# Third layer of a decoder: one drive in four of the state-space scan made by GpSimd, and its cross attention rewritten as one stage in slots

## The chip, the cores and the metric

The kernel runs on one core of one Trainium2 chip. Its time is the device time of one launch in microseconds (us). Engine names here are those of the profile: PE is TensorE, DVE is VectorE, ACT is ScalarE, POOL is GpSimd and SP is SyncE. PSUM is the memory that matmuls write, SBUF the other on-chip memory. POOL has no operand in PSUM anywhere in this kernel.

## The reference

A decoder of four layers works on `x` of 16 batches x 128 tokens x 128 features, with a context of 16 x 120 x 96. Each layer has a mixing block, a cross attention and a feed-forward block, and after each block `x = layernorm(x + block(x))`. The change touches two blocks of the third layer, L2:

```python
# L2_attn: selective state-space model, D_MODEL 128, D_INNER 256, D_STATE 64
x, z   = split(x @ in_proj)                 # x goes through a causal convolution, then silu
dt     = softplus(low_rank(x) @ dt_proj_w + dt_proj_b)
B, C   = two more projections of the input, 64 columns each
h_t[d,n] = exp(dt_t[d] * A[d,n]) * h_{t-1}[d,n] + (dt_t[d] * u_t[d]) * B_t[n]     # for each state n
y_t[d]   = sum_n h_t[d,n] * C_t[n] + D[d] * u_t[d]
out    = (y * silu(z)) @ out_proj
# L2_xattn: cross attention, 16 heads of 64
q, k, v = x @ Wq, ctx @ Wk, ctx @ Wv        # 1024 columns each
out     = softmax(q k^T / 8) v @ Wo + bo
```

## The kernel before

All work is in float32, apart from the split B and C rows of the state-space block, which are three bfloat16 parts. The 16 batches are taken in NG = 4 groups of G = 4 batches (4 x 128 tokens = 512 columns, `GT`). A *stage* is a block in which every engine runs its own instruction list, in order, and the lists meet only through semaphores; between two stages all engines meet.

**`l2_attn`** is one stage. Features lie on partitions, so one state n of one group is a tile of 128 x 1024 (two halves of D_INNER x 512 columns, `HW` = 1024). The stage walks k = 0 to 255 (group g = k // 64, state n = k % 64), and for each k:

- PE copies row n of B over 128 partitions into the PSUM bank `b_bank`, and row n of C into `c_bank` (`row(k, m)`, L3173), and adds the `read` tile of k - 2 into the PSUM total through an identity matmul (`add`, L3182).
- DVE multiplies `b_bank` by `du` (dt times u, in SBUF) into two PSUM banks, `drive_` (L3372), and then scans along the columns, `scan` (L3380): `state = decay * state + drive`. The scan reads `decay` from SBUF and the drive from PSUM.
- ACT moves the C row to SBUF (`c_move`, L3299, two buffers) and makes `exp(dt * a)` two states ahead (`decay_`, L3292, three buffers).
- POOL multiplies the scanned state by the C row (`read_`, L3477), from SBUF to SBUF.

In between, at fixed n, stand the pieces that finish the group before and prepare the next. On DVE: `skip` at n = 2 (L3388, twice), `moments` at n = 10 (L3394, L3398, L3400), `scale` at n = 12 (L3405), `split_rest` at n = 28, 31, 34 and 37 (L3357), `softplus_` at n = 52 (L3362: it reads two tiles, both in SBUF). On POOL: `gated` at n = 2, `rstd_` at 10, `split_low` at n = 29, 32, 35 and 38, and `delta_u` at 53.

**`l2_xattn`** first loads its weights in a stage of its own (`load`), then clears two tiles in another, then runs a hardware loop over the four groups. In one pass these stages follow each other: transposes of x and a copy of the context (`load_group`, `context_group`), projections (a stage with L1271 for q, L1273 for k and L1276 for v, c = 0 to 7), the attention core of 16 units of 4 heads each (scores L1227, maximum L323, subtraction L327, exponential L347, transposes of the weights L296, values L307, reciprocal and division L332 and L334), transposes of the output (L229), the output projection (L253, L256) and the layer norm (`finish_group`). K is kept with zeros in the other head's half, so that a score matmul uses 128 rows for one head's 64. V has a column of ones, from which the sum of the weights comes.

## Time and profile before

| what | value |
|---|---|
| median of three runs | 5960.31 us (5947.09 to 5963.47) |
| the profiled execution's own time | 5968.24 us |
| its span in the profile | 5966.5 us |
| busy in the span | PE 4702.8 us, DVE 4159.5, ACT 2844.0, POOL 2449.2 |
| mean granted clock of TensorE | 0.888 |

The profile is of one execution. The span is the time from its first instruction to its last, and the run's own time lies 1.7 us above it. The twelve blocks follow one another, so each block's time counts in full. The busy shares above are averages over blocks with different limits, and what an engine's time is worth has to be read inside the block.

### The profile page before, as it was taken

Reading aid. Unit: us, or ns where it says so; the run is one execution under the profiler, and the core shown is the slowest. Engines: PE = TensorE matmul, PEld = TensorE weight load, DVE = VectorE, ACT = ScalarE, POOL = GpSimd, SP = SyncE. Lnnn points to the kernel's source line nnn. Section 1 sums busy time; section 2 is a strip of 40 time slices with the busy share of each in tenths; the row PEclk is TensorE's granted clock in tenths of the full one; section 3 lists DMA queues with packets and bytes.
Section 4 is the critical chain, followed back from the end, with each engine's and each line's share of the span. In section 5 each row is a group of like instructions: output and inputs, shape, how many; then the busy total and the mean of one; then the engine's idle time right before and its main releaser. Section 6 shows DMA issues by size and latency. Waiting matters only on the chain. (4 is left out here: it accounts for less than half of the span.)

```text
span 5966.5 us, 85422 instructions
## 1 busy us (share of the span) xinstructions
PE 4702.8 (79%) x29391; PEld 2817.2 (47%) x29392; DVE 4159.5 (70%) x7865; ACT 2844.0 (48%) x4658; POOL 2449.2 (41%) x2180
## 2 busy tenths in 40 slices
PE   8768999999999999579537667666886689826667
PEld 5555666666666666237412222223563444304444
DVE  3338888888888887574459999996453446557545
ACT  2326777777777776444235454542233235413211
POOL 0137666767666665340546666662002210001100
PEclk8779999999999999778569999998897779966788
DMA  0000000000000000000000000000000000002000
GB/s 15 6 27 9 1 18 4 1 20 1 20 1 20 1 5 1 4 2 2 3 7 0 0 0 0 0 0 13 0 0 13 12 8 5 1 11 60 6 23 7
DMA packets 74746, 49.73 MB, mean 8 GB/s; under 512 B 27816, under 2 KB 68921, under 8 KB 73593
## 3 DMA queue, kind: packets, MB, share of 16 engines
q1 hardware_dynamic: 72313, 43.71, 2.8%
q8 instruction: 221, 3.62, 0.3%
q0 software_dynamic: 2048, 1.05, 0.1%
q14 instruction: 164, 1.34, 0.1%
HBM read 40.11 MB, written 1.18 MB: 7 GB/s over the span
## 5 line engine op out<-in xcount | busy, mean ns | idle before, releaser
L3477 POOL TENSOR_TENSOR l_attn_read<-l_attn_state,l_attn_c_rows 128x1024 f32<-128x1024 f32 x256 | 604.5, 2361 | 329.3 <-DVE l_attn_state L3380 328.4
L2354 POOL TENSOR_TENSOR l_ffn_t<-l_ffn_t 128x512 f32<-128x512 f32 x384 | 488.5, 1272 | 520.6 <-DVE l_ffn_t L2221 520.6
L3380 DVE TENSOR_TENSOR_SCAN l_attn_state<-l_attn_decay,psum 128x1024 f32<-128x1024 f32 x256 | 584.9, 2285 | 8.1
L1954 PE MATMUL psum<-l_ffn_wq,l_ffn_xsT 128*128 128x512 f32 x1152 | 562.7, 597 | 22.0 <-DVE l_ffn_t L2221 13.4
L3182 PE MATMUL psum<-l_attn_read,ident 128*128 128x512 f32 x1024 | 495.2, 606 | 5.4 <-DVE l_attn_yz L3388 3.0
L3173 PE MATMUL psum<-l_attn_parts,pick 96*128 96x512 bf16 x512 | 200.8, 396 | 309.9 <-DVE psum L3372 309.9
L2365 POOL TENSOR_TENSOR l_ffn_p<-l_ffn_p,l_ffn_sm 128x512 f32<-128x512 f32 x384 | 399.6, 1041 | 61.9 <-DVE l_ffn_sm L2253 45.5
L2360 POOL TENSOR_TENSOR l_ffn_t<-l_ffn_t,l_ffn_ss 128x512 f32<-128x512 f32 x384 | 400.9, 1044 | 0.7 <-DVE l_ffn_ss L2236 0.7
L3299 ACT COPY l_attn_c_rows<-psum 128x512 f32<-128x512 f32 x256 | 149.9, 586 | 469.2 <-PE psum L3173 467.7
L3372 DVE TENSOR_TENSOR psum<-psum,l_attn_du 128x1024 f32<-128x1024 f32 x256 | 315.6, 1233 | 32.4 <-POOL l_attn_du L3454 4.6
L2217 DVE TENSOR_TENSOR l_ffn_t<-psum,l_ffn_tab 128x512 f32<-128x512 f32 x384 | 263.4, 686 | 105.4 <-ACT l_ffn_sq L2101 103.6
L2118 ACT COPY l_ffn_pT<-psum 128x512 f32<-128x512 f32 x384 | 224.6, 585 | 217.5 <-PE psum L1984 214.1
L2112 ACT ACTIVATE l_ffn_p<-l_ffn_p 128x512 f32<-128x512 f32 x384 | 241.4, 629 | 150.7 <-DVE l_ffn_p L2244 148.3
L3173 PEld LDWEIGHTS psum<-l_attn_parts,pick 96*128 96x128 bf16 x512 | 50.0, 98 | 553.7 <-DVE psum L3372 480.9
L2240 DVE TENSOR_REDUCE l_ffn_mx<-psum 128x4 f32<-128x512 f32 x384 | 258.1, 672 | 68.4 <-PE psum L1975 66.3
L203 POOL TENSOR_SCALAR rstd<-mean_var 128x4 f32<-128x4 f32 x12 | 2.8, 231 | 734.9 <-DVE mean_var L192 734.9
L3292 ACT ACTIVATE l_attn_decay<-l_attn_dt,l_attn_a 128x1016 f32<-128x1016 f32 x256 | 292.7, 1144 | 11.8 <-DVE l_attn_state L3380 11.4
L1998 PEld LDWEIGHTS psum<-l_ffn_pT,l_ffn_v 128*64 128x64 f32 x3072 | 160.1, 136 | 280.3 <-issue 173.8
L1608 ACT ACTIVATE l_attn_pT<-psum 128x512 f32<-128x512 f32 x320 | 173.6, 594 | 243.1 <-PE psum L1506 170.6
L2101 ACT ACTIVATE l_ffn_sq<-psum 128x512 f32<-128x512 f32 x384 | 230.6, 600 | 121.1 <-PE psum L1954 121.1
L1975 PE MATMUL psum<-l_ffn_kT,l_ffn_qT 64*128 64x128 f32 x3072 | 274.9, 297 | 0.0
L2244 DVE TENSOR_TENSOR l_ffn_p<-psum,l_ffn_mx 128x512 f32<-128x512 f32 x384 | 265.6, 692 | 13.2
(884 smaller groups left out, 11896.1 us busy)
## 6 DMA issues: line engine op xcount, KB each, us to landing
l_ffn_wq<-in_L_ffn_Wqkv SPq DMA_DIRECT2D x6, 1536.0 KB, 6.6
l_xattn_toep<-s4d_taps SPq DMA_DIRECT2D x4, 2048.0 KB, 17.4
l_ffn_wo<-in_L_ffn_Wo SPq DMA_DIRECT2D x6, 512.0 KB, 8.3
l_ffn_w<-in_L_ffn_W SPq DMA_DIRECT2D x6, 341.0 KB
l_ffn_w<-in_L_ffn_w SPq DMA_DIRECT2D x3, 512.0 KB, 5.8
l_attn_k<-l_attn_dense_k POOLq DMA_DIRECT2D x64, 16.0 KB, 1.8
l_attn_q<-l_attn_dense_q SPq DMA_DIRECT2D x64, 16.0 KB
l_xattn_conv_y<-l_xattn_conv_rows SPq DMA_DIRECT2D x64, 16.0 KB, 2.2
```

The source lines that it names most:

```text
L1954: nc.tensor.matmul(ring[it % 2], xsT[:, n % 2, m % G, :], wq[:, z, i * 512:(i + 1) * 512], start=True, stop=True).then_inc(itemed, 1)
L1975: last = nc.tensor.matmul(S[:, par, i, :], qT[r, m % G, 2 * c + i, :], kT[r, m % G, 2 * c + i, :], start=False, stop=True, skip_group_chec ...
L2217: nc.vector.tensor_tensor(t1[:, m % G, i, :].rearrange("p (h d) -> p h d", d=dh), dots.rearrange("p (h d) -> p h d", d=dh), rows(tab[:, z, ...
L2244: nc.vector.tensor_tensor(p_[:, k % 4, :, :].rearrange("p (i par) t -> p par i t", par=2), S, mx[:, k % 2, :, :].unsqueeze(3).to_broadcast ...
L2354: nc.gpsimd.tensor_tensor(t1[:, m % G, i, :], t1[:, m % G, i, :], t2[:, x % 3, :], ALU.add).then_inc(added, 1)
L2360: nc.gpsimd.tensor_tensor(t1[:, m % G, i, :].rearrange("p (h d) -> p h d", d=dh), t1[:, m % G, i, :].rearrange("p (h d) -> p h d", d=dh), ...
L2365: nc.gpsimd.tensor_tensor(p_[:, k % 4, :, :], p_[:, k % 4, :, :], col(sm[:, k % 4, :], T), ALU.mult).then_inc(weighted, 1)
L3182: last = nc.tensor.matmul(total[:, h * GT:(h + 1) * GT], K.ident[:], read[:, k % 3, h * GT:(h + 1) * GT], start=(n == 0), stop=(n == N - 1 ...
L3292: nc.scalar.activation(decay[:, k % 3, :, :, 1:T], dt[:, g % 2, :].rearrange("p (h g t) -> p h g t", h=2, g=G)[:, :, :, 1:T], ACT.Exp, sca ...
L3372: nc.vector.tensor_tensor(drive.rearrange("p (h n) -> p h n", h=2), rows(b_bank, 2), du[:, g % 2, :].rearrange("p (h n) -> p h n", h=2), A ...
L3380: nc.vector.tensor_tensor_scan(state[:, k % 3, :], decay[:, k % 3, :, :, :].rearrange("p h g t -> p (h g t)"), drive, 0.0, ALU.mult, ALU.a ...
L3477: nc.gpsimd.tensor_tensor(read[:, k % 3, :].rearrange("p (h n) -> p h n", h=2), state[:, k % 3, :].rearrange("p (h n) -> p h n", h=2), row ...
```

## The change

In `l2_attn`, for states with n % 4 == 2 (16 per group, 64 in all) the drive is no longer made by DVE. PE makes the B row in `c_bank` (`b_row_copied`), ACT moves it to SBUF (`b_move`), POOL multiplies it by `du` into a new SBUF tile `drive_sb` (`drive_here`), and the scan of that state takes its drive from there. `drive_here(k + 2)` stands on POOL right behind `read_(k)` with k % 4 == 0. Nothing else in the stage is changed.

```diff
+        by_pool = lambda k: k % N % 4 == 2
```

On PE (`b_row` and `c_row` are what `row(k, 0)` and `row(k, 1)` were):

```diff
+                def b_row_copied(k, c_done):
+                    g, n = k // N, k % N
+                    if n < 3:
+                        wait_parts(g)
+                    if c_done:
+                        pe.wait_ge(c_moved, c_done)
+                    nc.tensor.matmul(c_bank, K.pick3[:, n % SU:n % SU + 1].to_broadcast([96, 128]), parts[:, g % 2, n // SU, :],
+                                     start=True, stop=True).then_inc(b_copied_ready, 1)
...
-                    if k + 1 < NS:
-                        row(k + 1, 0)
+                    if k + 1 < NS and not by_pool(k + 1):
+                        b_row(k + 1)
                     if k >= 2:
                         add(k - 2)
                     if k + 1 < NS:
-                        row(k + 1, 1)
+                        c_row(k + 1)
+                    if k + 3 < NS and by_pool(k + 3):
+                        b_row_copied(k + 3, k + 2)
```

On ACT, and then on DVE:

```diff
                     c_move(k)
+                    if k >= 1 and k + 2 < NS and by_pool(k + 2):
+                        b_move(k + 2)
                     if k + 2 < NS:
                         decay_(k + 2)
...
-                    dve.wait_ge(driven, k + 1)
+                    p = pool_index(k)
+                    if by_pool(k):
+                        dve.wait_ge(pool_driven, p + 1)
+                    else:
+                        dve.wait_ge(driven, dve_index(k) + 1)
...
-                    nc.vector.tensor_tensor_scan(state[:, k % 3, :], decay[:, k % 3, :, :, :].rearrange("p h g t -> p (h g t)"), drive, 0.0,
+                    nc.vector.tensor_tensor_scan(state[:, k % 3, :], decay[:, k % 3, :, :, :].rearrange("p h g t -> p (h g t)"),
+                                                 drive_sb[:, p % 2, :] if by_pool(k) else drive, 0.0,
                                                  ALU.mult, ALU.add).then_inc(scanned, 1)
...
-                    drive_(k)
+                    if not by_pool(k):
+                        drive_(k)
```

On POOL:

```diff
+                def drive_here(k):
+                    g, p = k // N, pool_index(k)
+                    pool.wait_ge(b_copied, p + 1)
+                    pool.wait_ge(du_ready, g + 1)
+                    if p >= 2:
+                        pool.wait_ge(scanned, prior_pool(prior_pool(k)) + 1)
+                    nc.gpsimd.tensor_tensor(drive_sb[:, p % 2, :].rearrange("p (h n) -> p h n", h=2), du[:, g % 2, :].rearrange("p (h n) -> p h n", h=2),
+                                            rows(b_rows[:, p % 2, :], 2), ALU.mult).then_inc(pool_driven, 1)
...
                     read_(k)
+                    if k >= 1 and k + 2 < NS and by_pool(k + 2):
+                        drive_here(k + 2)
```

On DVE, in the state-space stage, before (L3372 makes a drive, the L3380 rows are scans; both write or read the drive in PSUM):

```order
L3372 TENSOR_TENSOR psum<-psum,l_attn_du 128x1024
L3380 SCALAR_TENSOR_TENSOR l_attn_state<-l_attn_decay,psum 128x1024
L3372 TENSOR_TENSOR psum<-psum,l_attn_du 128x1024
L3380 SCALAR_TENSOR_TENSOR l_attn_state<-l_attn_decay,psum 128x1024
L3372 TENSOR_TENSOR psum<-psum,l_attn_du 128x1024
```

And of the change at the same place (L3640 is the drive, L3652 the scan), for k = 4j + 1, 4j + 2 and 4j + 3:

```order
L3640 TENSOR_TENSOR psum<-psum,l_attn_du 128x1024
L3652 SCALAR_TENSOR_TENSOR l_attn_state<-l_attn_decay,psum 128x1024
L3652 SCALAR_TENSOR_TENSOR l_attn_state<-l_attn_decay,l_attn_drive_sb 128x1024
L3640 TENSOR_TENSOR psum<-psum,l_attn_du 128x1024
L3652 SCALAR_TENSOR_TENSOR l_attn_state<-l_attn_decay,psum 128x1024
```

The drive of 4j + 2 is gone from DVE, and the scan behind it has both its inputs, `decay` and `drive_sb`, in SBUF.

On POOL, at the start of the same stage, of the change (L3722 is `split_low`, L3729 `delta_u`, L3762 `drive_here`, L3752 `read_`; before, 30 `read_` follow the `delta_u` without a break):

```order
L3722 TENSOR_TENSOR l_attn_parts<-l_attn_rest,l_attn_low 32x512 x4
L3729 TENSOR_TENSOR l_attn_du<-l_attn_dt,l_attn_xz 128x1024
L3762 TENSOR_TENSOR l_attn_drive_sb<-l_attn_du,l_attn_b_rows 128x1024
L3752 TENSOR_TENSOR l_attn_read<-l_attn_state,l_attn_c_rows 128x1024 x5
L3762 TENSOR_TENSOR l_attn_drive_sb<-l_attn_du,l_attn_b_rows 128x1024
L3752 TENSOR_TENSOR l_attn_read<-l_attn_state,l_attn_c_rows 128x1024 x4
```

The second `drive_here` stands behind `read_(4)` and ahead of `read_(5)`, and so on every fourth.

`l2_xattn` becomes one stage for all four groups. A slot t works on the pair of heads c = t % 8 of group t // 8 for all four batches (32 pairs; slots from -3 to 36). Scores use 64 rows of PE for each head, the two heads of a pair in two PSUM banks (`score`, 8 matmuls). The softmax keeps queries on partitions; the weights are normalised on POOL before they are transposed (`weigh`), and the value matmul writes the output transposed, so that the transposes of L229 fall away. The next group's q, k and v projections are spread over the slots, one of each per slot. The layer norm's multiply and add move from DVE to POOL (`norm`). The tiles that had to be cleared are gone, and the weights are loaded in the same stage.

```diff
-        with nc.Fori(0, NB // G) as i:
-            b0 = i * G
-            load_group(K, b0)
-            context_group(K, b0)
...
-            core()
-            wide_out(K, o, oT, wo, bo[:])
-            finish_group(K, b0)
...
+        def misc_at(t):
+            out = []
+            for g in range(NG):
+                u = t - CH * g + 2
+                if 0 <= u < CH:
+                    out += [("q", g, u), ("k", g, u), ("v", g, u)]
+            for g in range(NG):
+                if t == CH * g - 3:
+                    out.append(("x", g))
+                if t == CH * g + 11:
+                    out.append(("fin", g))
+            return out
```

Each engine's slot, in the order of its list: PE does value(t - 3), the q projection, score(t), the k projection, turn(t - 2), the v projection, and then "x" or "fin". ACT does move_out(t - 3), the moves of q and k, move(t - 2, 0) and move(t - 2, 1), the moves of v and x, exp(t, 0) and exp(t, 1). DVE does sums(t - 1) (two reduce_sum of 128 x 480 and a reciprocal), then shift(t, 0) and shift(t, 1) (reduce_max and subtraction each). POOL does weigh(t - 1) (two multiplications of 128 x 480). The waits that tie them:

```diff
+                def score(n):
+                    g, c = divmod(n, CH)
+                    if n:
+                        pe.wait_ge(shifted, 2 * n)
...
+                def turn(n):
+                    pe.wait_ge(weighted, 2 * n + 2)
+                    if n:
+                        pe.wait_ge(p_moved, 2 * n)
...
+                def value(n):
+                    g, c = divmod(n, CH)
+                    pe.wait_ge(p_moved, 2 * n + 2)
+                    if n:
+                        pe.wait_ge(o_moved, n)
...
+                    for b in range(G):
+                        for z in range(2):
+                            last = nc.tensor.matmul(O[half(z), b * T:b * T + T], v[:, g % 2, b, (2 * c + z) * dh:(2 * c + z + 1) * dh],
+                                                    pT[:, n % 2, z, b * T:b * T + T], start=True, stop=True, skip_group_check=True)
+                    last.then_inc(o_done, 1)
```

"fin" is the output projection of a group: 32 matmuls of 128 x 128.

On PE, in the cross attention, one slot of the change (L1329 `value`, L1348 q, L1305 `score`, L1351 k, L1316 `turn`, L1355 v; x8 stands for eight matmuls):

```order
L1329 MATMUL psum<-l_xattn_pT,l_xattn_v 64x128 x8
L1348 MATMUL psum<-xT,l_xattn_wq 128x512
L1305 MATMUL psum<-l_xattn_k,l_xattn_q 128x120 x8
L1351 MATMUL psum<-ctxT_all,l_xattn_wk 128x480
L1316 MATMUL psum<-ident,l_xattn_p 120x128 x8
L1355 MATMUL psum<-l_xattn_wv,ctxT_all 120x512
```

Before, 24 projections stand together in front of the core, and one unit of the core is this:

```order
L1227 MATMUL psum<-l_xattn_kT,l_xattn_qT 128x2x120 x2
L296 MATMUL psum<-ident,l_xattn_l2x_p 120x128 x4
L307 MATMUL psum<-l_xattn_v,l_xattn_l2x_pT 128x65 x4
L1227 MATMUL psum<-l_xattn_kT,l_xattn_qT 128x2x120 x2
L296 MATMUL psum<-ident,l_xattn_l2x_p 120x128 x4
```

A slot stands for two units. The projections now lie between its parts.

## Rows read from the trace of the kernel before

**Rows 1.** Stretches: length, busy of PE, PEld, DVE, ACT, POOL, granted clock, DMA.

```profile
3109.00:4073.00 964.00, 661.47 (x1691) 255.00 (x1692) 927.61 (x572) 479.14 (x594) 633.70 (x282) 0.98 0.00 0
4114.00:4472.00 358.00, 300.08 (x1648) 227.42 (x1648) 199.44 (x412) 113.80 (x196) 5.07 (x8) 0.91 0.00 0
```

**Rows 2.** Timeline (start, duration, engine, line, names) of one state-space step.

```profile
4062.09 2.37 POOL L3477 TENSOR_TENSOR l_attn_read<-l_attn_state,l_attn_c_rows 128x1024 f32<-128x1024 f32 x1 [1.30 <-DVE l_attn_state L3380]
4062.11 1.23 DVE L3372 TENSOR_TENSOR psum<-psum,l_attn_du 128x1024 f32<-128x1024 f32 x1
4063.38 2.29 DVE L3380 TENSOR_TENSOR_SCAN l_attn_state<-l_attn_decay,psum 128x1024 f32<-128x1024 f32 x1
...
4063.63 1.88 PE L3182 MATMUL psum<-l_attn_read,ident 128*128 128x512 f32 x4
...
4065.74 2.35 POOL L3477 TENSOR_TENSOR l_attn_read<-l_attn_state,l_attn_c_rows 128x1024 f32<-128x1024 f32 x1 [1.29 <-DVE l_attn_state L3380]
...
4065.77 1.23 DVE L3372 TENSOR_TENSOR psum<-psum,l_attn_du 128x1024 f32<-128x1024 f32 x1
```

**Rows 3.** Timeline at n = 52, where DVE's `softplus_` meets a running `read_`.

```profile
3300.14 2.35 POOL L3477 TENSOR_TENSOR l_attn_read<-l_attn_state,l_attn_c_rows 128x1024 f32<-128x1024 f32 x1 [1.30 <-DVE l_attn_state L3380]
...
3301.31 2.27 DVE L3362 SCALAR_TENSOR_TENSOR l_attn_dt<-l_attn_dt,l_attn_tmp 128x1024 f32<-128x1024 f32 x1
```

**Rows 4.** The four instances of line L3362: shortest, median, longest in ns.

```profile
L3362 DVE SCALAR_TENSOR_TENSOR l_attn_dt<-l_attn_dt,l_attn_tmp x4: 1226/2270/2282, 3102.3 to 3787.9; 128x1024 f32<-128x1024 f32 x4
```

**Rows 5.** Timeline in the second layer: POOL's L3017 releases DVE's L2939.

```profile
2531.73 1.04 POOL L3017 TENSOR_TENSOR rstd<-rstd,minus_half 128x4 f32<-128x4 f32 x1
...
2532.74 1.27 POOL L3024 TENSOR_TENSOR l_attn_read<-l_attn_state,l_attn_c_rows 128x512 f32<-128x512 f32 x1
...
2532.87 1.75 DVE L2939 TENSOR_SCALAR x_all<-y,mean_var,rstd 128x128 f32<-128x128 f32 x3
```

**Rows 6.** DVE's groups of instructions in the state-space stage (count | busy us, mean ns).

```profile
L3357 DVE TENSOR_TENSOR l_attn_rest<-psum,l_attn_parts 96x512 f32<-96x512 f32 x13 | 8.8, 678 | 1.3 <-POOL l_attn_parts L3447 1.3
...
L3388 DVE SCALAR_TENSOR_TENSOR l_attn_yz<-l_attn_xz,l_attn_cl,psum 128x512 f32<-128x512 f32 x8 | 5.6, 741 | 4.5 <-PE psum L3182 4.5
L3398 DVE BATCH_NORM_STATS2 stats<-y 128x6 f32<-128x128 f32 x16 | 4.7, 294 | 0.5
```

**Rows 7.** Timeline: first instructions of the cross attention, and the next block's first.

```profile
4091.63 0.34 SPq L92 DMA_DIRECT2D l_xattn_wq<-in_L_xattn_Wq  x1
...
4101.94 3.52 DVE L1253 MEMSET l_xattn_v<- 120x4160 f32 x1 [12.35 <-PEq L42]
...
4117.70 2.05 PE L1271 MATMUL psum<-xT,l_xattn_wq 128*128 128x512 f32 x2 [2.07 <-PEq L39]
...
4473.03 0.35 SPq L92 DMA_DIRECT2D l_ffn_gate<-in_L_ffn_gate_w  x1
```

**Rows 8.** Timeline of projections in the third group: two turns of q, k and v.

```profile
4303.67 1.02 PE L1271 MATMUL psum<-xT,l_xattn_wq 128*128 128x512 f32 x2
...
4306.19 1.02 PE L1271 MATMUL psum<-xT,l_xattn_wq 128*128 128x512 f32 x2
```

**Rows 9.** Timeline of PE in the first layer's feed-forward block, which runs in slots.

```profile
1800.06 0.66 PE L1998 MATMUL psum<-l_ffn_pT,l_ffn_v 128*64 128x128 f32 x8
...
1800.65 0.66 PE L1960 MATMUL psum<-ident,l_ffn_t 128*128 128x128 f32 x4
...
1802.31 0.71 PE L1975 MATMUL psum<-l_ffn_kT,l_ffn_qT 64*128 64x128 f32 x8
...
1802.96 0.66 PE L1984 MATMUL psum<-ident,l_ffn_p 128*128 128x128 f32 x4
...
1803.45 1.88 PE L1954 MATMUL psum<-l_ffn_wq,l_ffn_xsT 128*128 128x512 f32 x4
```

**Rows 10.** Timeline of the output projection in the third group, one batch.

```profile
4368.25 2.02 PE L253 MATMUL psum<-l_xattn_wo,l_xattn_oT 128*128 128x128 f32 x16 [1.27 <-PEq L42]
```

**Rows 11.** DVE's groups of instructions in the cross attention (count | busy us, mean ns).

```profile
L327 DVE TENSOR_TENSOR l_xattn_l2x_p<-psum,l_xattn_l2x_max 128x480 f32<-128x480 f32 x64 | 42.1, 658 | 2.2
```

More of the change, by code:

```diff
@@ L1250, in l2_xattn @@
-        with stage(nc) as (block,):
+        wo = sb("wo", [128, CH, D])
+        bo = sb("bo", [128, D])
+        x_bias = sb("x_bias", [128, G, D])
+        q = sb("q", [128, CH, GT])
+        k = sb("k", [128, CH, KEYS])
+        v = sb("v", [NC_, 2, G, E])
+        p_ = sb("p", [128, 3, 2, G, NC_])
+        mx, sm = sb("mx", [128, 2, G]), sb("sm", [128, 2, 2, G])
+        pT = sb("pT", [NC_, 2, 2, GT])
+        oT = sb("oT", [128, 2, CH, GT])
+        st, mv = sb("st", [128, G, 6]), sb("mv", [128, G, 2])
@@ new lines, in l2_xattn @@
+        rs, nb = sb("rs", [128, G]), sb("nb", [128, G])
+        xT = K.xT[:].rearrange("p g t -> p (g t)")
+        O = K.bank[4]
+        spare = [K.bank[5 + i] for i in range(3)]
+        half = lambda z: slice(64 * z, 64 * z + 64)
+        def misc_at(t):
[10 more added lines that the diff above has]
+            return out
@@ new lines, in sums, with moments @@
+                def sums(n):
+                    for z in range(2):
+                        dve.wait_ge(exped, 2 * n + z + 1)
+                        if n >= 2:
+                            dve.wait_ge(weighted, 2 * (n - 2) + 2)
+                        nc.vector.reduce_sum(sm[:, n % 2, z, :], p_[:, n % 3, z, :, :], AX).then_inc(summed, 1)
+                    dve.wait_ge(summed, 2 * n + 2)
+                    nc.vector.reciprocal(sm[:, n % 2, :, :], sm[:, n % 2, :, :]).then_inc(recip, 1)
+                def moments(g):
+                    key = ("fin", g)
+                    wait_filled(dve, *key)
+                    dve.wait_ge(x_biased, g + 1)
+                    if g:
+                        dve.wait_ge(x_ready, g)
+                    nc.vector.tensor_tensor(K.y[:].rearrange("p g d -> p (g d)"), bank_of(key), x_bias[:].rearrange("p g d -> p (g d)"),
+                                            ALU.add).then_inc(moved[use[key] % 3], 1)
+                    wait_moved(dve, *key)
+                    for b in range(G):
+                        step(nc.vector.bn_stats(st[:, b, :], K.y[:, b, :]))
+                    if g:
+                        dve.wait_ge(rstd_ready, g)
+                    for b in range(G):
+                        nc.vector.bn_aggr(mv[:, b, :], st[:, b, :]).then_inc(var_ready, 1)
@@ L3196, in _ @@
                     dt_dot(0, h)
-                row(0, 0)
-                row(0, 1)
+                b_row(0)
+                b_row_copied(2, 0)
+                c_row(0)
                 for k in range(NS + 2):
                     g, n = k // N, k % N
-                    if k + 1 < NS:
-                        row(k + 1, 0)
+                    if k + 1 < NS and not by_pool(k + 1):
+                        b_row(k + 1)
                     if k >= 2:
@@ L3483, in _ @@
                 delta_u(0)
+                drive_here(2)
                 for k in range(NS):
```

284 lines of the change are left out of this document (227 added, 57 removed).

## The prediction

> **What bounds the kernel now.** I read the busy times of the two blocks first, then the timeline of one step in each. In the state-space steps DVE is busy 927.6 of 964 us [rows 1]; the reader is to see that no other engine is near that (PE 661, POOL 634, ACT 479). The timeline shows why: drive 1.23 us, scan 2.29 us, next drive, with gaps of 0.04 and 0.10 us between [rows 2]. One step is 3.66 us from drive to drive (4062.11 to 4065.77), four are 14.64. POOL starts its `read_` 0.07 us after a scan and is done 1.3 us before the next one is. So time taken off DVE here shortens the block, until POOL's chain is the longer one.
>
> The cross attention takes from 4091.63, where its first load is issued, to 4473.03, where the next block's first is [rows 7]: 381.4 us. Until 4117.70 it only loads, clears and transposes. In its four groups PE is busy 300 of 358 us and no other engine over 200 [rows 1]. PE has pauses only between stages. So what counts is PE's work, and the empty starts and ends of stages.
>
> **The state-space stage, step by step.** In words the change takes 64 drives of 1.23 us off DVE, which with their gap would be 64 x 1.37 = 88 us. I follow one cycle of four states, time 0 being the end of scan(4j), with the durations and gaps of [rows 2].
>
> - POOL: `read_(4j)` 0.07 to 2.43, `drive_here(4j + 2)` 2.39 to 4.75. It has no row of its own; I take 2.36 us, that of `read_`, which has the same shape and the same two SBUF inputs, one repeated over halves. Then `read_(4j + 1)` from 4.71, since its scan has long ended.
> - DVE: drive(4j + 1) 0.10 to 1.33, scan(4j + 1) 1.37 to 3.66. Then it waits for POOL's drive, until 4.82. That is the first loss: 1.16 us of the 1.37 gained.
> - The second loss is larger. scan(4j + 2) now has both inputs in SBUF, and starts 0.1 us behind a POOL instruction that reads SBUF. The trace has this pair: `softplus_` (two SBUF inputs) takes 1226 ns alone and 2270 ns in the middle of three others [rows 4]. At 3301.31 it starts while POOL's `read_` runs, until 3302.49; it ends at 3303.58, 1.09 us later [rows 3]. So it does nothing until POOL has finished, and then needs 0.14 us less than alone. Ordinary drives and scans, with one SBUF input, are not lengthened by a running `read_` [rows 2].
> - Who comes first is also in the trace. In the second layer POOL ends L3017 at 2532.77; its next instruction has already started, at 2532.74, while the DVE instruction that waited for L3017 starts at 2532.87, and its three operations end at 2534.62, 0.61 us behind that next POOL instruction (2534.01) [rows 5]. Here it is the same: `read_(4j + 1)` at 4.71, the scan at 4.82. So scan(4j + 2) waits to 7.07 and ends at 7.07 + 2.29 - 0.14 = 9.21.
> - Then two ordinary steps: 9.21 + 2 x 3.66 = 16.53. POOL is at rest before the next cycle starts, so it repeats.
>
> A cycle costs 16.53 - 14.64 = +1.89 us. For 63 of them (in the first, drive_here(2) is made ahead of everything) that is +119 us, and -1 in the first. What comes back: DVE now idles 3.4 us before every scan(4j + 2), and the pieces that stand there cost nothing: `skip` (2 x 0.74), `moments` (4 x 0.29, and about 1.1 for its addition and aggregations), two of four `split_rest` (0.68 each) [rows 6]. That is 4.9 us less overlaps of 0.1, 3 times: -14.5. At n = 32 `split_low` stands between `drive_here` and `read_`; there the scan already waits when POOL passes on, goes first, and saves 1.2 us, 3 times: -3.6. Sum of this stage: **+100 us**.
>
> The Trainium skill speaks against this change (SBUF — State Buffer, "Who interferes with whom"): a DVE instruction with two SBUF inputs contends with a GpSimd instruction that reads SBUF, and whichever issues first holds the shared ports for its whole length. By that rule, the trace agrees, with 2270 against 1226 ns. Without the rule the scan would start at 4.82, and the cycle be 14.42 us.
>
> PE, ACT: the B row for POOL costs PE 0.4 and ACT 0.6 us per cycle, and both have the room (PE 661 and ACT 479 of 964 us busy [rows 1]). PE's list is in order, and `b_row(4j + 4)` waits for drive(4j + 3), which ends at 10.54, so PE idles some 5 us in each cycle and then works through one copy of B, two additions of 1.9 us [rows 2] and three more copies. Worked through with the gaps above, the C row for `read_(4j + 4)` is moved at 14.0 (needed at 16.6), the B row for drive(4j + 5) is there at 14.9 (16.6), POOL's B row at 15.3 (18.9). I charge nothing; the cover is 1.7 us or more.
>
> **The cross attention.** PE's work per slot, start to start, each f32 matmul being two instructions except the transposes:
>
> - q, k, v: 2.52 us (4303.67 to 4306.19) [rows 8].
> - value, 16 instructions: eight of this kind take 0.59 us up to the next, of which 0.2 is the change of shape; 0.59 + 8 x 0.055 = 1.03. Scores, 16 of 64 rows: 0.65 + 8 x 0.063 = 1.15. Eight transposes: 0.49 + 4 x 0.11 = 0.93 [rows 9].
> - Changes of shape behind the projections: 0.17. Sum 5.8 us.
>
> `value(t - 3)` waits for ACT's second move of the slot before. The turn begins at 4.0, its halves are moved one after another, and the second is done at about 5.9: 0.1 us of wait. **5.9 us** a slot. The others stay below: DVE 2 x (0.66 + 0.66) + 2 x 0.66 + 0.2 = 4.2 by [rows 11]; ACT eight instructions of 0.6, 4.8; POOL 2 x 1.1, `read_`'s duration at 480 of 1024 columns.
>
> Start: DVE's first instruction behind the loads is at 4101.94 [rows 7], and PE no longer waits for the clearing; I put the first q at 4100.5. There q took 2.05 us for 1.02 later [rows 7, 8], so slots -2 and -1 cost 8 us instead of 5. Slots 0 to 2: 13.5, since they bring only part of the work but each score waits for the maximum and subtractions of the last. Slots 3 to 29: 27 x 5.9 = 159. Three output projections of 64 instructions in them: 2.02 us per 16 as read [rows 10], and a little less start to start, 3 x 7.7 = 23; transposes of x 1. Slots 30 and 31, bound by DVE: 8.6. The tail behind them (last exponential, sums, weights on POOL, turn, move, value, move: about 10; the last projection 8 to 12, its clock partly down; moments and the norm on POOL 6; the block's end 2): 29. Sum: 4100.5 + 8 + 13.5 + 159 + 24 + 8.6 + 29 = 4342.6, and 4473.0 before: **-130 us**. With slots of 5.8 and 6.3 us, -133 and -119; with a tail of 22 or 36, 7 either way.
>
> **Sum.** 5968.2 + 100 - 130 = 5938 against the profiled execution, which lies 7.9 us above the median shown. Against that median, 5960.3 - 30 = **5930 us**.
>
> **The rivals.**
>
> - *The scan is not held up* (DVE gets in first, or a scan does not share what `softplus_` shares). For it: no scan with two SBUF inputs is in the trace. Against: [rows 3 to 5]. The cycle is then 14.42 us, 64 x 0.22 = -14, and the stretches of 1.2 us before scan(4j + 2) hide 12: -26 in this stage, 5960 - 26 - 130 = 5804. Chance 0.10. The Trainium skill's page on SBUF makes no exception for scans.
> - *Slots bound by waits, not by PE.* ACT's eight instructions go round with PE's, and a wait that is not 0.1 but 1.1 us in each of 27 slots takes 27 us away: 5957, no change. For it: the value matmul waits for the last of a chain PE, ACT, PE inside one slot. Against: the feed-forward block has the same chain, and its PE rows stand close [rows 9]. Chance 0.16.
> - *Slower: PE's clock falls in the state-space stage.* Now it is 0.98 of 2.4 GHz there [rows 1] while PE is busy in each step; the change makes a pause of 5 us per cycle. With all of PE's work at 1.2 GHz, four steps take it 4 x (2 x 0.86 + 3.44) + 0.86 = 21.5 us, longer than the 16.53, and the stage would be 320 us longer still. Only part of the cycle behind the pause would be slow, and the cover of 1.7 us takes up most. Where 0.5 us per cycle is left over the gain is gone; from 0.8 the kernel is slower (+21 us, 5981). Chance 0.12.
> - *The forecast*, 0.62, with a range of its own from 5912 to 5952: the two losses as worked out, tail and slots within their bounds.
>
> **How the numbers follow.** What can be told from no change is about 0.3%, 18 us: the three runs of before lie 16 us apart. Faster than 5942: 0.53 of the forecast's 0.62, all of the first rival, a little of the second: 0.64. Slower than 5978: most of the third rival, the second's far end: 0.13. The rest, 0.23, lies between. The range from 5895 to 5975 leaves out the first rival at one end and the third's far part at the other.
>
> **What would show it.** In the state-space stage: scans of n % 4 == 2 with durations near 4.4 us and the others at 2.29; their starts 0.1 us behind a `read_` start; scan to scan over four states 16.5 us; the stretch of 964 us [rows 1] grown to about 1064. In the cross attention: PE without pauses, slots of 5.9 us, first q near 4200 with the stage before 100 us longer, 251 us in all. The prediction is wrong if those scans last 2.3 us, if the granted clock of the stage drops well below 0.9, or if the slot is over 6.5 us.

## The result, and the profile after

The kernel after takes **5926.06 us** (median of five runs, 5920.25 to 5929.68); the kernel before, beside it, 5957.74 us (five runs, 5947.09 to 5963.47). The ratio is **0.9947, interval 0.9933 to 0.9962**: a gain of 32 us where 30 were predicted. Its profiled execution took 5929.38 us with a span of 5927.6.

The two blocks went opposite ways. These are stretches of the kernel after: length, busy time of PE, PEld, DVE, ACT and POOL, granted clock. They answer to [rows 1].

```profile
3099.00:4164.00 1065.00, 753.70 (x1693) 294.04 (x1694) 965.88 (x508) 521.75 (x658) 803.67 (x347) 0.84 0.00 0
4190.00:4430.00 240.00, 224.87 (x1740) 151.35 (x1740) 134.20 (x260) 136.34 (x259) 80.28 (x100) 0.96 0.01 1
```

The state-space stretch grew from 964 to 1065 us. DVE has 64 instructions less in it and is busy for 38 us longer. The scan's line shows where that sits (shortest, median and longest in ns; first and last start in us):

```profile
L3652 DVE TENSOR_TENSOR_SCAN l_attn_state<-l_attn_decay,psum x192: 2270/2286/2287, 3099.2 to 4159.1; 128x1024 f32<-128x1024 f32 x192
L3652 DVE TENSOR_TENSOR_SCAN l_attn_state<-l_attn_decay,l_attn_drive_sb x64: 2265/4415/4435, 3105.0 to 4153.3; 128x1024 f32<-128x1024 f32 x64
```

It is the same instruction with the same shape. The reader is to see that only the place of its second input differs, PSUM or SBUF, and that the median goes from 2.29 to 4.42 us while the shortest does not. DVE's waits in this stretch (total us, times, longest):

```profile
DVE l_attn_state L3652 <- POOL l_attn_drive_sb L3762: 55.9, 52, 1.9
DVE psum L3640 <- PE psum L3410: 12.4, 17, 2.7
DVE psum L3640 <- POOL l_attn_du L3729: 4.6, 1, 4.6
```

One cycle in the timeline, DVE and POOL only (start, duration; in brackets the idle time before, and who ended it):

```profile
4067.30 2.29 DVE L3652 TENSOR_TENSOR_SCAN l_attn_state<-l_attn_decay,psum 128x1024 f32<-128x1024 f32 x1
4068.33 2.35 POOL L3762 TENSOR_TENSOR l_attn_drive_sb<-l_attn_du,l_attn_b_rows 128x1024 f32<-128x1024 f32 x1
4070.64 2.35 POOL L3752 TENSOR_TENSOR l_attn_read<-l_attn_state,l_attn_c_rows 128x1024 f32<-128x1024 f32 x1
4070.72 4.42 DVE L3652 TENSOR_TENSOR_SCAN l_attn_state<-l_attn_decay,l_attn_drive_sb 128x1024 f32<-128x1024 f32 x1 [1.13 <-POOL l_attn_drive_sb L3762]
...
4075.22 2.37 POOL L3752 TENSOR_TENSOR l_attn_read<-l_attn_state,l_attn_c_rows 128x1024 f32<-128x1024 f32 x1 [2.23 <-DVE l_attn_state L3652]
4075.24 1.23 DVE L3640 TENSOR_TENSOR psum<-psum,l_attn_du 128x1024 f32<-128x1024 f32 x1
```

The scan waits 1.13 us for POOL's drive. It then starts 0.08 us behind POOL's next `read_`, and ends 2.15 us after that read has ended (4075.14 against 4072.99). [rows 3] had 1.09 of 1.23 us in the same place for `softplus_`; both times the instruction needs 0.14 us less than alone once POOL is done.

The cross attention begins with its first load, its first q follows 10.2 us later, and the next block's first load ends it. So it takes 248.4 us, where [rows 7] had 381.4.

```profile
4180.03 0.35 SPq L1289 DMA_DIRECT2D l_xattn_wq<-in_L_xattn_Wq  x1
...
4190.22 2.08 PE L1348 MATMUL psum<-xT,l_xattn_wq 128*128 128x512 f32 x2 [9.06 <-DMA l_xattn_bo<-in_L_xattn_bo]
...
4428.45 0.34 SPq L92 DMA_DIRECT2D l_ffn_gate<-in_L_ffn_gate_w  x1
```

A stretch laid from one value stage to the next shows what sets the slot:

```profile
4300.71:4306.61 5.90, 5.90 (x47) 3.62 (x46) 3.95 (x8) 4.18 (x8) 1.94 (x3) 1.00 0.00 0
```

PE is busy for 5.90 of 5.90 us, at full clock; no other engine is above 4.2.

I add DVE's rows between the first and the last of the 256 scans, in each kernel. "Held" is what scans take above 2.286 us, "pieces" are the instructions that belong to neither drives nor scans, "waits" are idle times over 0.25 us, "gaps" the shorter ones. These are sums of mine over the traces, in us:

```
kernel                        stretch  scans  held   drives  pieces  waits  gaps
before                          961.3  582.9    0.0   314.4    33.8    1.4  29.2
after                          1060.0  582.9  117.0   235.5    33.7   71.3  19.8
e2_ssm_only                    1065.7  582.9  123.5   235.5    34.0   70.2  19.8
e4_port_alone                  1012.9  582.9   52.0   313.9    33.8    1.4  29.2
e5_drive_unused                 961.7  582.9    0.0   314.4    34.2    1.4  29.1
e3_drive_first (64 by POOL)     919.9  582.9   37.3   235.5    31.6   17.4  15.5
e7_three_of_16 (48 by POOL)     924.7  582.9   28.8   255.2    30.3    8.6  19.2
e9_spread (48 by POOL)          907.9  582.9   14.9   255.2    33.7    1.0  20.8
e6_eighth_first (32 by POOL)    918.1  582.9    4.7   275.0    30.4    2.8  23.0
```

From before to after: drives -78.9, gaps -9.4, held +117.0, waits +69.9, in all +98.5; the stretches differ by 98.7.

The two spans differ by -38.9 us: +98.7 here, -133.0 in the cross attention, +5.7 behind it, and -10.2 ahead of the first scan (it starts at 3099.2, before at 3109.4), where the two kernels have the same code. The last is no effect of the change: two profiles of one and the same kernel, e6_eighth_first and e10_eighth_again below, have their first scan at 3106.0 and at 3098.4.

### The profile page after: what moved, and what is told of

Its sections match the earlier page's. It is cut to its first block and busy times, and to the rows that moved or that the text cites. A ratio compares the mean times of both kernels' runs of the same rounds, so it can differ in the third digit from the quotient of the medians.

```text
span 5927.6 us, 85459 instructions
## 1 busy us (share of the span) xinstructions
PE 4708.5 (79%) x29488; PEld 2771.3 (47%) x29488; DVE 4121.7 (70%) x7647; ACT 2909.6 (49%) x4786; POOL 2691.5 (45%) x2336
## 3 DMA queue, kind: packets, MB, share of 16 engines
HBM read 40.18 MB, written 1.18 MB: 7 GB/s over the span
## 5 line engine op out<-in xcount | busy, mean ns | idle before, releaser
L3752 POOL TENSOR_TENSOR l_attn_read<-l_attn_state,l_attn_c_rows 128x1024 f32<-128x1024 f32 x256 | 611.2, 2390 | 258.8 <-DVE l_attn_state L3652 247.8
L3437 PE MATMUL psum<-l_attn_read,ident 128*128 128x512 f32 x1024 | 580.9, 696 | 19.3 <-POOL l_attn_read L3752 15.3
L3652 DVE TENSOR_TENSOR_SCAN l_attn_state<-l_attn_decay,psum 128x1024 f32<-128x1024 f32 x192 | 438.7, 2285 | 6.1
L3437 PEld LDWEIGHTS psum<-l_attn_read,ident 128*128 128x128 f32 x1024 | 224.7, 222 | 236.0 <-issue 191.0
L3652 DVE TENSOR_TENSOR_SCAN l_attn_state<-l_attn_decay,l_attn_drive_sb 128x1024 f32<-128x1024 f32 x64 | 263.3, 4114 | 56.0 <-POOL l_attn_drive_sb L3762 55.9
L2479 DVE TENSOR_REDUCE l_ffn_sm<-l_ffn_p 128x4 f32<-128x512 f32 x384 | 260.1, 677 | 19.0 <-ACT l_ffn_p L2340 15.0
L3410 PE MATMUL psum<-l_attn_parts,pick 96*128 96x512 bf16 x192 | 85.5, 446 | 232.7 <-DVE psum L3640 232.4
```

What stands on the lines that cost most here:

```text
L2479: nc.vector.reduce_sum(sm[:, k % 4, :], p_[:, k % 4, :, :], AX).then_inc(sum_ready, 1)
L3437: last = nc.tensor.matmul(total[:, h * GT:(h + 1) * GT], K.ident[:], read[:, k % 3, h * GT:(h + 1) * GT], start=(n == 0), stop=(n == N - 1 ...
L3652: nc.vector.tensor_tensor_scan(state[:, k % 3, :], decay[:, k % 3, :, :, :].rearrange("p h g t -> p (h g t)"), drive_sb[:, p % 2, :] if by ...
L3752: nc.gpsimd.tensor_tensor(read[:, k % 3, :].rearrange("p (h n) -> p h n", h=2), state[:, k % 3, :].rearrange("p (h n) -> p h n", h=2), row ...
```

## The experiments

My theory was that of the prediction. The scan that waits for POOL's drive gets it 1.1 us late, then meets POOL's next read and cannot run beside it; the cross attention is PE's work and takes 5.9 us a slot. Against it stood: the two halves are not independent; POOL's or PE's added work is the loss, not its use; a scan with two SBUF inputs is slow in itself; a slot is set by ACT's moves. Ratios are to the kernel before, on the same chip.

**Each half by itself.** `e1_xattn_only` is the kernel before with the new `l2_xattn`, `e2_ssm_only` the kernel before with the new `l2_attn`; nothing else is edited.

> The kernel before with the new third cross attention alone; the state-space stage as before. My theory: the two halves add up, so the cross attention's stretch is 248 us as in the kernel after (381 before), the state-space stretch from first to last scan stays at 961, and the time is about 133 us below the kernel before, near 5825 us, ratio 0.978. Rival (the halves are not independent: the short cross attention owes something to the state the stretch before leaves PE's clock and the weights in): the cross attention's stretch differs from 248 us by more than 8, and the ratio from 0.978 by more than 0.002.

> The kernel before with the new third-layer state-space stage alone; cross attention as before. My theory: first to last scan 1060 us for 961, the cross attention 381 us, and the time about 98 us above the kernel before, near 6056, ratio 1.0165. Rival (moving 64 drives off the busiest engine does save time in itself, and the stretch was long in the kernel after only because of what else was changed): the stretch is at or below 961 and the ratio at or below 1.000.

Measured: 5826.04 us, ratio 0.9776 (0.9761 to 0.9791), and 6064.35 us, ratio 1.0172 (1.0155 to 1.0188). The excesses add up: -2.24% and +1.72% are -0.52%, and both together gave -0.53%. In the first, the cross attention takes 243.0 us, from its first load to the next block's:

```profile
4089.81 0.34 SPq L1289 DMA_DIRECT2D l_xattn_wq<-in_L_xattn_Wq  x1
...
4332.81 0.34 SPq L92 DMA_DIRECT2D l_ffn_gate<-in_L_ffn_gate_w  x1
```

In the second, the 64 scans are as in the kernel after (held by 123.5 us for 117.0), and so nearly is the stretch (1065.7 for 1060.0). So the state-space half alone loses 109 us (98 expected), and the gain of the whole is what the cross attention leaves over. Both rivals fall: 243.0 is within 8 us of 248 and the ratio within 0.002 of 0.978, and the stretch is far above 961. Of the 5.4 us between 243.0 and 248.4, 1.2 lie ahead of the first q and 3.3 behind the start of the last value stage; there that stage takes 1.97 us and the output projection behind it 9.78, for 1.09 and 7.38 in `e1_xattn_only`, at a granted clock of 0.72 (4400.0 to 4428.4) for 0.90 (4304.4 to 4332.8). Why the clock differs there is open.

**Two SBUF inputs beside a running read, and nothing else.** `e4_port_alone` is the kernel before; in every fourth state DVE writes its own drive to SBUF (a new tile `drive_sb`) and the scan reads it there. POOL does only what it did before.

```diff
-                    nc.vector.tensor_tensor(drive.rearrange("p (h n) -> p h n", h=2), rows(b_bank, 2),
+                    to = drive_sb[:, k // 4 % 2, :] if k % 4 == 2 else drive
+                    nc.vector.tensor_tensor(to.rearrange("p (h n) -> p h n", h=2), rows(b_bank, 2),
...
-                    nc.vector.tensor_tensor_scan(state[:, k % 3, :], decay[:, k % 3, :, :, :].rearrange("p h g t -> p (h g t)"), drive, 0.0,
+                    nc.vector.tensor_tensor_scan(state[:, k % 3, :], decay[:, k % 3, :, :, :].rearrange("p h g t -> p (h g t)"),
+                                                 drive_sb[:, k // 4 % 2, :] if k % 4 == 2 else drive, 0.0,
```

> The kernel before, with one edit: for every fourth state (n % 4 == 2) DVE itself writes its drive to SBUF instead of PSUM, and the scan takes both inputs from SBUF. POOL's work is that of before, and no engine does anything more. Theory A (a scan with two SBUF inputs cannot run while POOL's read runs): read_(n-1) starts 0.07 us behind scan(n-1) and runs 2.36 us, the scan would start 1.3 us behind scan(n-1) and so is held until POOL is done: its duration is about 3.2 us for 2.29, +0.92 us x 64 = +59, less what the pieces between steps hide, about +51 us, near 6011, ratio 1.0085. Theory B (where the inputs lie does not matter, the loss in the kernel after is one of waiting alone): durations 2.29, ratio 1.000. Theory C (two SBUF inputs make a scan slow in itself): 4.4 us each, +137 us, ratio 1.023.

Measured: 6010.12 us, ratio 1.0083 (1.0069 to 1.0097), for 6011 and 1.0085 in theory A. Its scans, and one of them beside POOL's read, from the timeline:

```profile
L3382 DVE TENSOR_TENSOR_SCAN l_attn_state<-l_attn_decay,psum x192: 2272/2286/2287, 3108.5 to 4121.4; 128x1024 f32<-128x1024 f32 x192
L3382 DVE TENSOR_TENSOR_SCAN l_attn_state<-l_attn_decay,l_attn_drive_sb x64: 2255/3221/3236, 3115.8 to 4116.8; 128x1024 f32<-128x1024 f32 x64
```

```profile
3688.54 2.35 POOL L3480 TENSOR_TENSOR l_attn_read<-l_attn_state,l_attn_c_rows 128x1024 f32<-128x1024 f32 x1 [1.29 <-DVE l_attn_state L3382]
3689.82 3.22 DVE L3382 TENSOR_TENSOR_SCAN l_attn_state<-l_attn_decay,l_attn_drive_sb 128x1024 f32<-128x1024 f32 x1
```

POOL's read ends at 3690.89, the scan at 3693.04: again 2.15 us later. The time that the scan loses is what is left of POOL's instruction, less 0.14. A scan slow in itself would show 4.4 us here too, so theory C falls, and so does theory B (2.29 us). By the Trainium skill (SBUF — State Buffer, "Who interferes with whom"), a DVE instruction with two SBUF inputs contends with a GpSimd one that reads SBUF; the scan agrees, with 3221 ns for 2286.

**The load without its use.** `e5_drive_unused`: POOL, PE and ACT do all that the change adds, DVE makes its own drives and scans from PSUM.

```diff
-        dve_index = lambda k: k - pool_index(k)
+        dve_index = lambda k: k
...
-                    if k + 1 < NS and not by_pool(k + 1):
+                    if k + 1 < NS:
                         b_row(k + 1)
...
-                    p = pool_index(k)
-                    if by_pool(k):
-                        dve.wait_ge(pool_driven, p + 1)
-                    else:
-                        dve.wait_ge(driven, dve_index(k) + 1)
+                    dve.wait_ge(driven, dve_index(k) + 1)
...
-                                                 drive_sb[:, p % 2, :] if by_pool(k) else drive, 0.0,
+                                                 drive, 0.0,
...
-                    if not by_pool(k):
+                    if True:
                         drive_(k)
```

> The kernel after, but DVE makes all 256 drives itself and every scan reads its drive from PSUM; POOL still makes its 64 drives into SBUF, and PE and ACT still bring it the B rows, but nobody uses the result. It separates the load that the change adds (POOL, PE, ACT) from its use. Theory A (the load costs nothing; both losses come from scans that wait for POOL's drive and read it from SBUF): first to last scan 961 us as in the kernel before, all scans at 2.29 us, time near 5827 us as with the cross attention alone, ratio 0.978. Theory B (POOL, at 11.8 us of work per cycle of 14.6, or PE with the extra B rows, is itself too slow): the stretch is 975 us or more, the ratio 0.981 or more.

Measured: 5824.27 us, ratio 0.9774 (0.9758 to 0.9790), equal to the cross attention alone; stretch 961.7, all 256 scans between 2253 and 2289 ns. 64 more POOL instructions of 2.36 us, 64 more B rows and 64 more moves cost nothing: theory A, and theory B (975 us or more) falls. It also shows that running POOL reads and drives did not lengthen these scans, which have one input in SBUF.

**POOL's drive ahead of its read.** `e3_drive_first` is the kernel after with two lines exchanged.

```diff
                 for k in range(NS):
                     g, n = k // N, k % N
-                    read_(k)
                     if k >= 1 and k + 2 < NS and by_pool(k + 2):
                         drive_here(k + 2)
+                    read_(k)
```

> The kernel after with two lines exchanged: in each fourth state POOL makes the drive of two states ahead before its read, not behind it. Theory A (both losses are one of placing: POOL's drive is late, and the scan that waited for it then queues behind POOL's next read): the drive is done before DVE asks for it; what is behind it on POOL is read_(4j), which a DVE scan with two SBUF inputs may still meet. By the durations of the trace the cycle of four states then takes 13.8 us (16.5 in the kernel after, 14.6 before), the stretch from first to last scan about 880 to 900 us, and the time is near 5765 us, ratio 0.968, with the cross attention of the kernel after unchanged at 248 us. Theory B (a scan with two SBUF inputs is slow in itself, 4.4 us, whatever POOL does): scans of n % 4 == 2 still take 4.4 us, the cycle about 15.4 us, the time near 5870. Theory C (only the wait for the drive matters): scans of n % 4 == 2 all at 2.28 us, cycle 13.3 us, time near 5735.

Measured: 5788.68 us, ratio 0.9714 (0.9696 to 0.9732), 137 us below the kernel after, 24 above my number, and the stretch is 919.9 us for 880 to 900 expected. DVE no longer waits for POOL's drive at all. The scans:

```profile
L3652 DVE TENSOR_TENSOR_SCAN l_attn_state<-l_attn_decay,l_attn_drive_sb x64: 2265/2657/4231, 3112.1 to 4022.1; 128x1024 f32<-128x1024 f32 x64
```

and an undisturbed cycle, where POOL's two reads lie in one row:

```profile
3990.91 2.35 POOL L3762 TENSOR_TENSOR l_attn_drive_sb<-l_attn_du,l_attn_b_rows 128x1024 f32<-128x1024 f32 x1
3991.60 1.23 DVE L3640 TENSOR_TENSOR psum<-psum,l_attn_du 128x1024 f32<-128x1024 f32 x1
3992.86 2.29 DVE L3652 TENSOR_TENSOR_SCAN l_attn_state<-l_attn_decay,psum 128x1024 f32<-128x1024 f32 x1
3993.23 6.63 POOL L3752 TENSOR_TENSOR l_attn_read<-l_attn_state,l_attn_c_rows 128x1024 f32<-128x1024 f32 x2
3995.07 2.65 DVE L3652 TENSOR_TENSOR_SCAN l_attn_state<-l_attn_decay,l_attn_drive_sb 128x1024 f32<-128x1024 f32 x1
```

`read_` begins at 3993.23, right behind the drive, and takes 2.34 us, to 3995.57; the scan comes at 3995.07 and lasts 0.37 us longer than alone. Neither rival holds: the median of the 64 scans is 2.66 us, where theory B had 4.4 and theory C 2.28 for all. This cycle takes 13.54 us, a little less than the 13.8 expected. The miss is in the other cycles: 17.4 us of waits, 13.7 of them for PE's B row, and scans held by up to 1.95 us wherever POOL is further behind; 12 of the 64 scans are not held at all.

**What is still held.** The next kernels keep the drive ahead of the read and change only which states POOL serves: every eighth; three of 16; three of 16 in even steps. The count in `pool_index` follows; it is left out of the lines here.

```diff
-  by_pool = lambda k: k % N % 4 == 2
+  by_pool = lambda k: k % 8 == 2                        # e6_eighth_first, e10_eighth_again
+  by_pool = lambda k: k % 4 == 2 and k % 16 != 14       # e7_three_of_16
+  by_pool = lambda k: k % 16 in (2, 7, 12)              # e9_spread
```

> As e3_drive_first (POOL's drive ahead of its read), but POOL makes only every eighth state's drive. It asks why e3's stretch was 920 us where the sum had 880 to 900. Theory A (in e3 POOL and the held scans fill the cycle: five POOL operations of 2.36 and one scan of 2.27 that excludes them make 14 us of the 13.5, so nothing is left to hide the pieces between steps, and they cost about 53 us in all for 26 before): here POOL has room in every second cycle, the stretch is 32 x (13.54 + 14.64) + 26 = 928 us, time near 5797. Theory B (the pieces cost more because of what is done to the order, not for want of room on POOL): 32 x (13.54 + 14.64) + 53 = 955 us, time near 5824.

Measured: 5781.77 us, ratio 0.9704 (0.9688 to 0.9720), stretch 918.1. Half as many drives gain as much as e3's 64. The table says why: 39.5 us more of drives stay on DVE, but 4.7 us are held instead of 37.3 and 2.8 of waits instead of 17.4. Theory B (955 us) falls, and even theory A had 10 us too much, and 15 in the time. It held each of the 32 scans by 0.37, 11.8 us in all; 9 of them are held, for 4.7 us. That is 7 of the 10.

> As e3_drive_first, but POOL makes the drive of three of every 16 states (n % 4 == 2 without n % 16 == 14). Theory A (POOL's room hides the pieces between steps): 48 cycles of 13.54 and 16 of 14.64 make 884, and with 26 to 40 us for the pieces 910 to 924 us from first to last scan, time near 5779 to 5793, at or a little below e3_drive_first. Theory B (room on POOL is not what matters, each drive taken off DVE is worth its 1.1 us): 884 + 53 = 937 us, time near 5806, slower than e3_drive_first.

Measured: 5788.88 us, ratio 0.9720 (0.9704 to 0.9736), stretch 924.7: at theory A's far end (924), level with e3 in time, and 12 us below theory B's 937. Of the 16 scans with n % 16 = 2, which come after a rest, 10 take under 2.3 us; of the 32 that follow them only two do. In the first cycle of the stage one can see what such a scan does to POOL:

```profile
3111.00 2.27 DVE L3651 TENSOR_TENSOR_SCAN l_attn_state<-l_attn_decay,l_attn_drive_sb 128x1024 f32<-128x1024 f32 x1
3111.16 4.24 POOL L3751 TENSOR_TENSOR l_attn_read<-l_attn_state,l_attn_c_rows 128x1024 f32<-128x1024 f32 x1 [1.22 <-DVE l_attn_state L3651]
```

The scan came first this time, and POOL's read is the one that takes 4.24 us for 2.36. So each drive costs POOL its 2.36 us and about 1.9 for the scan that reads it. POOL is behind after that, and in the middle of a read when the next such scan comes.

> As e7_three_of_16 (48 of 256 drives by POOL, ahead of its read), but spread evenly: n % 16 of 2, 7 and 12 instead of 2, 6 and 10. In e7 the first drive of each run of three was mostly not held (scan 2.27 us, cycle 13.16), the second and third mostly were (2.65 us and more). Theory A (a drive costs POOL 2.36 us, and the scan that reads it keeps POOL out for 2.3 more; with only three other states between, POOL has not caught up and is in the middle of a read when the scan comes, with four it has): most of the 48 scans at 2.27 us, the sum above 2.29 us at most 10 us for e7's 28.8, first to last scan near 900 to 906 us, time near 5766. Theory B (what holds the scans is their place among the pieces of each group, not POOL's arrears): the sum above 2.29 stays at 20 to 30 us, the stretch near 925, the time near 5789.

> The kernel of e6_eighth_first once more, beside e9_spread on the same chip, to compare the two directly. Theory A of e9_spread: this one is 12 to 18 us slower than e9_spread. Theory B: 7 us faster. By itself: stretch 918 us, ratio 0.970.

Measured: 5775.55 us, ratio 0.9691 (0.9677 to 0.9706), and 5780.81 us, ratio 0.9702 (0.9687 to 0.9718). One state more between the drives cuts the held time from 28.8 to 14.9 us and the stretch from 924.7 to 907.9, though not to 10 and 906, and the time is 5776 for 5766. Of the 48 scans 29 take under 2.3 us. In the last group, which has no pieces for a next one, it is 11 of 12, for 3 of 12 in e7; in the three groups before it 18 of 36. So the even steps free scans, as theory A has it, but most of what is still held stands in the groups with pieces: theory B has a part in it. A scan after a pause, POOL's read just over:

```profile
3125.78 2.36 POOL L3761 TENSOR_TENSOR l_attn_drive_sb<-l_attn_du,l_attn_b_rows 128x1024 f32<-128x1024 f32 x1
3127.14 1.23 DVE L3639 TENSOR_TENSOR psum<-psum,l_attn_du 128x1024 f32<-128x1024 f32 x1
3128.09 2.34 POOL L3751 TENSOR_TENSOR l_attn_read<-l_attn_state,l_attn_c_rows 128x1024 f32<-128x1024 f32 x1
3128.41 2.29 DVE L3651 TENSOR_TENSOR_SCAN l_attn_state<-l_attn_decay,psum 128x1024 f32<-128x1024 f32 x1
3130.62 2.27 DVE L3651 TENSOR_TENSOR_SCAN l_attn_state<-l_attn_decay,l_attn_drive_sb 128x1024 f32<-128x1024 f32 x1
```

It is the fastest kernel here, 183 us below before and 150 below after. Its lead over every eighth is 5 us where theory A had 12 to 18. The intervals overlap, so the time alone does not show a lead; the stretches, one trace of each, differ by 9.5 us (907.9 and 917.4). Both kernels are clearly below before and after.

**What the slot hangs on.** `e8_turn_last` moves one projection ahead of the transposes in PE's list of the cross attention.

```diff
+                    for key in todo:
+                        if key[0] == "v":
+                            other(key)
                     if 0 <= t - 2 < PAIRS:
                         turn(t - 2)
                     for key in todo:
-                        if key[0] in ("v", "x", "fin"):
+                        if key[0] in ("x", "fin"):
                             other(key)
```

> The kernel after, with one change of order on PE in the cross attention: the v projection of a slot is issued ahead of the eight transposes, not behind them. PE's work is the same; what is taken away is the 1.0 us of matmul that lies over ACT's two moves of pT. Theory A (the slot is PE's work, 5.9 us, because the v projection covers the moves): value now waits about 1.0 us for the second move in each slot, the slot is 6.9 us, +29 us over the slots, the cross attention 277 us for 248, time near 5955, ratio 1.000. Theory B (the slot is set by something else on ACT or DVE with room to spare on PE): the slot stays 5.9 us, the time near 5926, ratio 0.995.

Measured: 5946.5 us, ratio 0.9981 (0.9972 to 0.9991); the slot is 6.70 us and the cross attention 262.6. PE's rows around its new wait, and its waits in all:

```profile
4304.52 1.02 PE L1355 MATMUL psum<-l_xattn_wv,ctxT_all 96*120 96x512 f32 x2
4305.38 1.04 PE L1316 MATMUL psum<-ident,l_xattn_p 128*120 128x128 f32 x8
4306.02 1.07 ACT L1397 COPY l_xattn_pT<-psum 120x512 f32<-120x512 f32 x2 [0.74 <-PE psum L1316]
4307.14 1.09 PE L1329 MATMUL psum<-l_xattn_pT,l_xattn_v 120*64 120x128 f32 x16 [0.73 <-ACT l_xattn_pT L1397]
```

```profile
PE psum L1329 <- ACT l_xattn_pT L1397: 20.3, 29, 1.2
```

It goes theory A's way, with a smaller size: 0.8 us a slot for 1.0, and the block 14.2 us longer for 29. By the medians it is 20 us; the trace is of the fastest of ten runs (5936.95). The slots that hold an output projection did not grow (13.05 us from value stage to value stage in both kernels). The same work in another order costs that much because nothing covers ACT's moves; in the kernel after the v projection does, and PE does not pause. Theory B falls.

## Why the prediction was right

By its steps, with what was measured:

- **POOL's drive late.** Predicted 1.16 us in each ordinary cycle; measured 1.13 in the one shown, 55.9 us in 52 waits. Predicted for all of it: 63 x 1.16 less the 14.5 hidden behind pieces, 58.6. Right. (The pieces listed for that term add up to 5.1 us a group, not 4.9; that is 0.6 us in all.)
- **The scan held.** Predicted an end at 9.21 for a start at 4.82, so 4.39 us; measured 4.42. Held time predicted 63 x 2.10 - 3.6 = 129, measured 117. Seven scans of 64 took under 2.3 us where I had four, and three more, at n = 10, where `moments` makes DVE late, were held by 0.07, 0.98 and 1.03 us. e4 shows the mechanism alone, e3 to e9 that it goes with POOL's place.
- **Cycle and stretch.** 16.53 us predicted, and the median from scan to scan over four states is 16.53. Stretch +100 predicted, +98.7 measured. The first rival (scan not held, 0.10) is out.
- **PE and its clock.** I charged nothing, and named a granted clock well below 0.9 as a sign that the prediction is wrong. It is 0.84, for 0.98 in [rows 1], and DVE waits 12.4 us for PE's B row. So this term was mis-sized: 12 us instead of 0. It hardly shows in the sum, because the held scans came out 12 us below their term. Half of that is PE's lateness itself. Three times DVE had waited for the B row two states ahead of its scan of POOL's drive (1.18, 1.16 and 2.74 us, at n = 44, 16 and 36). So it came to that scan just as POOL finished the drive and not before, the scan began ahead of POOL's next read, and 3 x 2.13 us of holding fell away. That it cancels so nearly is luck. In `e2_ssm_only`, with the same stage, the two are 7.5 us of waiting and 123.5 held. The third rival's mechanism is real, but 0.2 us per cycle, not 0.5 or more. Its sum for a stage all at the lower clock was too high as well: it counts a copy of a row at 0.86 us, and below one takes 0.41 up to the next instruction (4076.53 to 4076.94), which makes 17.5 us of the 21.5, still above 16.53. This is what it looks like behind PE's pause:

```profile
4076.53 0.61 PE L3410 MATMUL psum<-l_attn_parts,pick 96*128 96x512 bf16 x1 [4.91 <-DVE psum L3640]
4076.94 3.62 PE L3437 MATMUL psum<-l_attn_read,ident 128*128 128x512 f32 x4
...
4081.89 0.38 PE L3410 MATMUL psum<-l_attn_parts,pick 96*128 96x512 bf16 x1
```

  After 4.91 us of idling the B row takes 0.61 us where the same row takes 0.38 later, and four matmuls of the addition take 3.62 where [rows 2] has 1.88. The granted clock from 4074.3 to 4081.1 is 0.50, the lower level of 1.2 GHz. The cover of 1.7 us was enough in most cycles.
- **Load on PE, ACT and POOL at nothing.** Shown right by e5: 5824.27 us for 5826.04.
- **The slot.** 5.9 us predicted, 5.90 measured, PE busy in all of it. Made up a little differently: I had 5.8 of work and 0.1 of wait, and it is 5.9 of work. Three of the slots take 6.34, and one with an output projection 7.15 more than the others where I had 7.7. The second rival (0.16) is out; e8 shows what it would have cost, 0.8 us a slot.
- **Start and tail.** From the first load to the first q 8.9 us predicted, 10.2 measured, with PE waiting for the bias row's transfer until the end. The tail from the last score is 30.1 us (4398.35 to 4428.45), for 29. From the first q to the last score it is 208.1 us, for 213.1. The block 248.4 for 251: start and tail took 2.4 us more than predicted, what lies between 5 less.

## What to carry to other kernels

An operation moved from the bottleneck engine to another is worth its time only if the result arrives early and in a place from which the bottleneck engine can read it freely. Here 88 us of DVE's work were moved and the stretch grew by 99 us all the same, by the order of two lines on POOL and by an input that lay in SBUF instead of PSUM. When the helper's instructions can hold up the engine that it helps, try asking for less help: with POOL making 64 drives 52 of their scans were held, with 32 drives 9. Half the drives gained as much as all of them, and 48 in even steps gained 17 us more in the stretch than 48 in runs of three. And split a change that has two halves: its +109 and -129 us would have passed for one small gain.

## What the runs showed of the hardware

- The exclusion works both ways, and costs the later one what is left of the earlier one's instruction: a scan of 2.29 us took 4.42, 3.22 or 2.65 us by its start behind POOL's read, and POOL's read took 4.24 for 2.36 where it started 0.16 us behind such a scan (e7).
- At the end of a POOL instruction the order is decided by who is already waiting. A scan already issued gets in between two POOL instructions (e3: it is there at 3995.07, in the middle of `read_`, and ends 2.15 us after that read; POOL's second read of the row starts at 3995.53 and takes 4.33 us). A scan that is only released by the end of a POOL instruction comes too late: POOL's next had started 0.08 us ahead of it (4070.64 and 4070.72).
- PE's granted clock over the stretch fell with a change in its pauses, not in its busy share. Before, PE is busy 661 of 964 us and the clock is 0.98 [rows 1]; after, 754 of 1065 us, and it is 0.84. By sums of mine over the traces PE idles as long in both, 301 and 307 us between the first and the last scan, but the pauses over 2 us are 11 before (3.0 us on average) and 54 after (4.3). PE's waits for a drive of DVE, ahead of the B row, are these before, in the kernel after and in e3, whose clock is 0.94:

```profile
PE psum L3173 <- DVE psum L3372: 309.9, 244, 11.5
```

```profile
PE psum L3410 <- DVE psum L3640: 232.4, 66, 5.9
```

```profile
PE psum L3410 <- DVE psum L3640: 67.1, 55, 3.6
```

  Pauses of 3.5 us on average went with the lowest clock. But 1.3 us before and 1.2 in e3 went with 0.98 and 0.94, and e4, with 42 pauses over 2 us, has 0.95, so their length does not explain all of it. No run changed the pauses alone: the cause is a reading here, not shown.
